# Moving a kernel's tokens and output rows by a table of row numbers: two batches and one output through GpSimd's indirect transfers, one batch at offsets in registers

## The reference, cut to what matters

```
x  = L0_attn_x
xn = layernorm(x)
x  = x + L0_attn(xn) + L0_ffn(xn)
#   L0_attn: 16 heads of 64, attention over channels: softmax(q k^T * 8) v, then w_out
#   L0_ffn:  64 experts of inner width 88, 8 chosen per token, and a shared expert: silu(x Wg) * (x Wu), then Wd
xn = layernorm(x)
x  = x + L1_attn(xn) + L1_ffn(xn)
#   L1_attn: for each of 8 heads the 32 nearest of the last 64 positions, weighted by exp(-distance)
#   L1_ffn:  relu(x W1 + low rank)^2, then W2, with ternary weights
return x
```

## Time and profile before

| | before |
|---|---|
| median time of 2 runs | 679.18 us (678.78 to 679.58) |
| span of the profiled execution | 676.3 us |
| instructions in it | 14256 |
| moved by transfers | 15.81 MB, nearly all in the first 45 us |

### The profile page before, as it was taken

One profiled execution on the slowest core, in us unless ns is written; L12 is line 12 of the kernel. 1 busy time (PEld: TensorE's weight loads), 2 busy tenths in 40 slices (PEclk: granted clock), 3 DMA queues, 4 the chain that ended last, 5 costly groups with the idle time before them and its releaser, 6 DMA issues.

```text
span 676.3 us, 14256 instructions
## 1 busy us (share of the span) xinstructions
PE 638.7 (94%) x4792; PEld 430.7 (64%) x4792; DVE 545.1 (81%) x2461; ACT 444.6 (66%) x802; POOL 365.4 (54%) x448
## 2 busy tenths in 40 slices
PE   4887999999999999999999999999999999998886
PEld 3544766667656666767567567666567776675675
DVE  5987778645975999997976899965485999967997
ACT  3674454646787957448587786455888956467953
POOL 2278366566462787665452886653763576621220
PEclk9999999999999999999999999999999999999999
DMA  8940000000000000000000000000000000000000
GB/s 297 392 131 1 0 1 0 1 0 1 0 1 1 2 2 1 1 1 1 2 0 2 2 1 2 1 1 1 1 1 1 2 1 1 1 1 17 18 18 17
DMA packets 12968, 15.81 MB, mean 23 GB/s; under 512 B 1728, under 2 KB 10832, under 8 KB 12384
## 3 DMA queue, kind: packets, MB, share of 16 engines
q1 hardware_dynamic: 12896, 14.91, 6.3%
HBM read 13.85 MB, written 1.05 MB: 22 GB/s over the span
## 4 chain that ended last, share of the span: by engine, by line
PE 61%; DVE 24%; ACT 7%; POOL 4%; issue 3%; DMA 0%; DVEq 0%; POOLq 0%; ACTq 0%
PE bank_A L522 17%; PE bank_U L522 14%; PE bank_G L522 14%; PE bank_X L522 14%; DVE Wk L1278 6%; DVE m L1275 5%; DVE S L859 4%; DVE GWk L859 2%; POOL PR L1654 2%; ACT L1350 1%; PE bank_X L531 1%; ACT Ed L1345 1%; PE bank_X L825 1%; ACT PR L1345 1%; ACT L1345 1%
## 5 line engine op out<-in xcount | busy, mean ns | idle before, releaser
L1654 POOL TENSOR_TENSOR Wlo<-Wgu,Whi 128x256 fp32r<-128x256 f32 x184 | 134.9, 743 | 119.5 <-ACT Whi L1345 116.5
L522 PE MATMUL bank_A<-S,WdT 128*128 128x512 f32 x346 | 172.2, 599 | 0.2 <-POOL S L1654 0.2
L1654 POOL TENSOR_TENSOR S<-S,Rb 128x512 f32<-128x512 f32 x84 | 108.6, 1294 | 72.0 <-DVE S L859 71.4
L859 DVE TENSOR_TENSOR S<-S,bank_U 128x512 f32<-128x512 f32 x173 | 116.6, 684 | 37.5 <-PE bank_U L522 23.3
L1345 ACT ACTIVATE Whi<-Wgu 128x256 fp32r<-128x256 f32 x184 | 73.0, 413 | 53.0 <-PE bank_U L522 48.5
L522 PE MATMUL bank_G<-xH,Whi 128*128 128x512 f32 x184 | 94.7, 515 | 8.0 <-POOL Wlo L1654 3.8
L522 PE MATMUL bank_U<-xH,Whi 128*128 128x512 f32 x184 | 93.4, 508 | 1.6 <-DVE wT L859 1.1
L522 PEld LDWEIGHTS bank_A<-S,WdT 128*128 128x128 f32 x346 | 61.7, 189 | 34.6 <-issue 21.4
L1278 DVE MATCH_REPLACE8 Wk<-m,Wk 128x79 f32<-128x79 f32 x384 | 82.2, 226 | 0.0
L1345 ACT ACTIVATE bank_G<-bank_G 128x512 f32<-128x512 f32 x83 | 48.4, 583 | 42.9 <-PE bank_G L522 42.6
L1345 ACT ACTIVATE S<-bank_G 128x512 f32<-128x512 f32 x90 | 53.7, 596 | 34.3 <-PE bank_G L522 27.5
(11 more groups left out here) (294 smaller groups left out, 1176.0 us busy)
## 6 DMA issues: line engine op xcount, KB each, us to landing
Wgu<-in_Wgu SPq DMA_DIRECT2D x2, 2048.0 KB, 14.4
xs<-in_x SPq DMA_DIRECT2D x4, 256.0 KB, 6.0
wqk<-in_w_qkv SPq DMA_DIRECT2D x1, 1024.0 KB, 6.9
Wgu<-in_Wgu SPq DMA_DIRECT2D x1, 1024.0 KB, 9.5
out<-xs SPq DMA_DIRECT2D x3, 256.0 KB, 2.3
Wgu<-in_Wgu SPq DMA_DIRECT2D x1, 512.0 KB, 4.7
wout<-in_w_out SPq DMA_DIRECT2D x1, 512.0 KB, 8.1
wvT<-in_wvT SPq DMA_DIRECT2D x1, 512.0 KB, 9.2
```

Of the source, the lines that this page charges most:

```text
L522: return engine.matmul(dst, lhsT, rhs, start=start, stop=stop)
L859: return engine.tensor_tensor(dst, a, b, op)
L1654: return engine.tensor_tensor(dst, a, b, op)
```

## The change

A table `rows` of shape (128, 16), the numbers 0 to 2047 in uint32, comes in as an input and is loaded into the tile `rowno`: column c holds the numbers of the 128 rows of tile c.

- Batch 1: SyncE reads the first row number of each of the four tiles from `rowno` into a register and issues one transfer of 64 KB at that offset; VectorE waits for 64 on `ld_x1`.
- Batch 2: GpSimd issues four indirect transfers, each of 128 rows named by a column of `rowno`.
- Batch 3: GpSimd zeroes batch 3's part of `xs` (ident minus ident), and later issues four indirect transfers that add the rows to it.
- Batch 0's output: four indirect transfers of GpSimd write the rows; SyncE stores batches 1 to 3 as before.
- SyncE no longer loads batches 2 and 3 and no longer stores batch 0.

```diff
@@ ORDER["pool"]: x and o are new letters (fetch three times, rows_out once)
-        "llylllllalmmlllmaaaclacalamlllmalmllmllmyylmlllmllmllmllmlymlllmmllmlllmlllmllmllmllmlylylmlllmllmll"
+        "llylllllalmmlllmaaaclacalamlllmalmllmllmyylmlllmllmllmllmlymxlllmmlxlmlllmxlllmllmllmllmlylylmlllmll"
...
+        rowno = sb("rowno", [128, B * NT], mybir.dt.uint32)
...
             load("ld_c", cst[:, :], d["consts"])
+            load("ld_r", rowno[:, :], d["rows"])
...
             load_w(2)
-            load_x(1)
+            sp.wait_ge("ld_r", 16)
+            for i in range(NT):
+                at = engine.value_load(rowno[0:1, NT + i:NT + i + 1], min_val=0, max_val=B * T - 128)
+                load("ld_x1", xs[:, NT + i, :], d["x"].rearrange("b t c -> (b t) c")[bass.ds(at, 128), :])
             load_w(3)
             load_w(4)
-            load_x(2)
-            load_x(3)
...
             def store(b, i, n):
                 j = i + n - 1
+                if b == 0:
+                    return
...
-            sp.wait_ge("st_out", 16 * (B - 1 + NT))
+            sp.wait_ge("st_out", 16 * (B - 2 + NT))
+            sp.wait_ge("st_rows", 16 * NT)
...
-                dve.wait_ge(f"ld_x{b}", 16)
+                dve.wait_ge(f"ld_x{b}", 16 * NT if b > 0 else 16)
...
+            def rows_of(b, i):
+                return bass.IndirectOffsetOnAxis(ap=rowno[:, NT * b + i:NT * b + i + 1], axis=0)
+
+            def fetch():
+                x = d["x"].rearrange("b t c -> (b t) c")
+                for b in (2, 3):
+                    if b == 3:
+                        yield
+                        po.wait_ge("ld_c", 16)
+                        one = K("ident").unsqueeze(1).to_broadcast([128, NT, 128])
+                        tt(xb(b), one, one, ALU.subtract).then_inc(sems("x_zero"), 1)
+                    yield
+                    po.wait_ge("ld_r", 16)
+                    if b == 3:
+                        po.wait_ge("x_zero", 1)
+                    for i in range(NT):
+                        engine.indirect_dma_start(
+                            out=xs[:, NT * b + i, :], out_offset=None, in_=x[:, :], in_offset=rows_of(b, i),
+                            **({"compute_op": ALU.add} if b == 3 else {})).then_inc(sems(f"ld_x{b}"), 16)
+
+            def rows_out():
+                o = out.rearrange("b t c -> (b t) c")
+                yield
+                po.wait_ge(empty(bank("dec", 0, NT - 1)), nth("dec", 0, NT - 1) + 1)
+                po.wait_ge(empty(bank("ff2", 0)), nth("ff2", 0) + 1)
+                for i in range(NT):
+                    engine.indirect_dma_start(
+                        out=o[:, :], out_offset=rows_of(0, i), in_=xs[:, i, :], in_offset=None).then_inc(sems("st_rows"), 16)
```

More of the change, by code:

```diff
@@ L71 @@
     "pool":
-        "llylllllalmmlllmaaaclacalamlllmalmllmllmyylmlllmllmllmllmlymlllmmllmlllmlllmllmllmllmlylylmlllmllmll"
-        "mhllmlymhlllmllmlmllmlaqllmqallaamqllamplalamlqllmlmlmqlplalmllqmlqlmllmlpmllqllmllmylylplmlhllmlmly"
-        "mhllllmmllllaqllaammlaqmlmlalaqlalmlapmllqmlqlmllmllqmplllmlqmllmlmllqllpmlllmlamplhlaaamallaalmlmha"
-        "lllmlmllmllqmlllqlmlqmllmlplmqlllmqmlllpmllqmllmqmlllpmmqphhhqqqqqqqq",
+        "llylllllalmmlllmaaaclacalamlllmalmllmllmyylmlllmllmllmllmlymxlllmmlxlmlllmxlllmllmllmllmlylylmlllmll"
+        "mllmhllmlymhlllmllmlmllmlaqllmqallaamqllamplalamlqllmlmlmqlplalmllqmlqlmllmlpmllqllmllmylylplmlhllml"
+        "mlymhllllmmllllaqllaammlaqmlmlalaqlalmlapmllqmlqlmllmllqmplllmlqmllmlmllqllpmlllmlamplhlaaamallaalml"
+        "mhalllmlmllmllqmlllqlmlqmllmlplmqlllmqmlllpmllqmllmqmlllpmmqphhohqqqqqqqq",
 }
@@ L1779, in every @@
                     yield from part(b)
-            weave("pool", c=zeros(), l=splits(), m=tiles(), y=every(route), a=every(attend), h=every(head), q=every(weights), p=adds())
+            weave("pool", c=zeros(), x=fetch(), o=rows_out(), l=splits(), m=tiles(), y=every(route), a=every(attend), h=every(head), q=every(weights), p=adds())
         block = ctx.enter_context(nc.Block())
@@ L1827 @@
         "x": i["L0_attn_x"],
+        "rows": np.arange(B * T, dtype=np.uint32).reshape(B * NT, 128).T,
         "consts": constants(),
```

## The result

| | before | changed |
|---|---|---|
| median time of 2 runs | 679.18 us | 698.16 us (696.70 to 699.63) |
| ratio | | 1.028, 95% interval 1.022 to 1.033 |
| span of the profiled execution | 676.3 us | 698.1 us |
| TensorE's hole ahead of chunk 32 / of chunk 40, as the ledger below counts it | none | 5.2 / 6.4 us |

The changed kernel is 19.0 us slower, 2.8%. Forecast were 10.8 us; the time lies inside the range, near its top. Run once more beside other runs of the kernel before it took 698.00 us, ratio 1.027 (1.025 to 1.030).

The account below looks back on a forecast made before the run. TensorE was taken as the bound from 100 to 610 us, so holes add to the time. First place 5.0, second 4.1 and clock 1.7 sum to 10.8 us on 679.2: 690.0 us, range 682.5 to 701.

Parts of the forecast that it names:

- D: Time for which one indirect transfer holds GpSimd; taken as 1.29 us, between ends of 0.44 and 2.35.
- First place: Batch 2's four transfers between product S3 and the Wlo of chunk 32; TensorE loses 5.0 us.
- (a): At chunk 32, GpSimd's hold makes Wlo late, so TensorE is late by 4D - 0.20, 4.96 us.
- (b): At route(2), VectorE's bn_stats wait for all four batch 2 transfers to land, making TensorE late by 4.76 us.
- cheap rival: GpSimd's transfers: issuing is nearly free (D = 0.44), about 2.3 us in all, 681.5 us; chance 0.20.
- Second place: Batch 3's four adding transfers after product S1, before the Wlo of chunk 40; 4D - 1.10, +4.1 us.
- Clock: TensorE's granted clock falls behind the holes; one drop counted, +1.7 us, none and two kept for the range.
- Zeroing: GpSimd's pass over batch 3's tile, 1.29 us, hidden in 2.58 us of idle time before a Wlo; cost 0.
- Output rows: Batch 0's four stores on GpSimd between hg and hq, with room for 3.25 us; cost 0 up to D = 1.65.
- SyncE's queue: Early table load and batch 1's register reads and four issues on SyncE, hidden; cost 0.
- Rival 1: GpSimd holds each transfer much longer (D = 2.35, or adding ones dearer), with two clock drops: 702.9 us; chance 0.30.
- Rivals 2, 3 and 4: 2: issuing nearly free, 681.5 us, chance 0.20; 3: slow SyncE register reads, 696.8, 0.03; 4: faster, 665.6, 0.01.

Follow-up runs that it names:

- e11: Kernel before with only batch 2's tokens by GpSimd's four indirect transfers, 64 rows each, SyncE loading the other halves; 686.99 us, ratio 1.0111.
- e2: Kernel before with only batch 3's part of the change: the zeroing and four adding transfers, placed as in the changed kernel; 689.01 us, ratio 1.0141.
- e12: Kernel before with only batch 3's zeroing and four adding transfers, one ahead of each of four Wlo; 683.51 us, ratio 1.0050.
- e14: All of the change, with the table loaded later and GpSimd's zeroing and batch 2 and 3 transfers moved to later waits than in an earlier idle-places version; 678.90 us, ratio 0.9997.
- e3: Kernel before with only batch 0's output rows stored by GpSimd's four indirect transfers; 679.25 us, ratio 0.9999.
- e5: Kernel before with only batch 3's tokens by GpSimd at the changed kernel's place, copying instead of adding, without zeroing; 683.07 us, ratio 1.0073.
- e13: Kernel before with only two tiles of batch 2 by GpSimd's indirect transfers, SyncE loading the other two; 682.94 us, ratio 1.0061.

## Why the prediction was right, and where it was off

The time lies in the range, but on its upper side: slower by more than 2% had a chance of 0.33, within 2% of 0.66. The range reached that far through its edge (D = 2.2 and two drops), so part of its being right is luck; two terms were mis-sized and two were put at nothing.

**First place.** Forecast 4D - 0.20 with D = 1.29, so +5.0; measured 5.17, 5.14, 5.08 and 5.10 in four profiles, D = 1.285. The slack of 0.20 was hardly there: 0.14 us lie between the end of Wlo and the matmul in the changed kernel too (122.88, 123.02). That the nearest row, GpSimd's pass over 128x512, gave D to a hundredth is luck: e11 shows that it isn't a cost per element or row. The choice of (a) over (b) was right, with the landing 1.5 us behind the last issue (122.12 to 123.60) for the 1.6 assumed. The Trainium skill's rule (DMA: Bandwidth & Descriptors, Anatomy of one DMA — SWDGE (gpsimd) path) of a small time for descriptors would have made this place nearly free; the trace disagrees for GpSimd's own time, and the prediction's cheap rival falls with it.

**Second place.** Forecast 4D - 1.10 = +4.1 "if adding costs GpSimd no more than copying". It does: 0.59 a transfer, so 6.4. With copying the step holds (4.20). This is the first mis-sized term, 2.3 us.

**Clock.** "I count one drop, +1.7 us", with two for the range. There were two, of 2.4 and 1.9: 4.3, so 2.6 us more than forecast, mostly for the second drop. The size came from a hole of 2.07 us ahead of other work; behind the holes of 4.9 to 6.6 us a drop cost 1.3 to 2.6, over eight holes in six profiles. The step also read from one profile that the hole of 2.61 us at 57.28 keeps the fast level; in nine of fourteen profiles the same hole lost it, and the hole of 2.07 us itself lost it in only five of the eleven profiles that have it.

**Zeroing.** Forecast 0, as hidden in GpSimd's idle time. GpSimd's time was hidden; what was overlooked is VectorE, which it blocked for 0.8 us ahead of a chunk whose Wlo had nothing to spare: 0.6.

**Output rows, SyncE's queue.** Forecast 0 and 0; measured alone 0.2 and 0.4 us with intervals that hold zero. Right, but for the open 2.3 us near the end, which come up only in the changed kernel. In its profile SyncE's later long issue is 6.57 us for the 9.79 of before, so the delay did come out of that standing.

**Sum.** 5.2 + 6.4 + 4.3 + 0.6 = 16.5, and with the open 2.3 it is 18.8, against 19.0 and 18.7 measured. That it comes so near is no proof of the 2.3: the parts measured alone give 18.6 without it, because their medians hold variation (e2's is 9.9 where its profile has 8.5). The forecast's 10.8 lacked 2.3 for adding, 2.6 for the clock, 0.6 for the zeroing and the 2.3 of the end. Rival 1 (a longer hold, 702.9) has half the truth: "the adding ones dearer" and "two drops" are in it, D = 2.35 isn't. Rivals 2, 3 and 4 fall by D = 1.285, by a read of about 0.8 us, and by the result.

## What to carry to other kernels

A transfer that GpSimd issues costs GpSimd its own time, about 1.3 us for each instruction here, with 64 rows as with 128, and 0.6 more if it adds; look for what GpSimd owes other engines in that time. Put such steps where the trace shows the engine idle and the next product early: the same change cost 18.7 us with two blocks of transfers ahead of late products, and nothing that could be told at idle places. Where TensorE is the bound, each hole of 4.9 us or more here cost 1.3 to 2.6 us again by the clock. Four transfers spread over four chunks (e12) lost 2.4 us where one block lost 7.9, hole and clock together; most of that is slack that each chunk has of its own. And a pass in an engine's idle time can still block another engine, as the zeroing did VectorE.

## What the runs showed of the hardware that I had not expected

- An indirect transfer takes GpSimd 0.95 us plus 0.30 between two, for 128 rows of 512 bytes as for 64 (0.90); the first of a block takes 1.17. Adding: 1.54 to 1.75 in the record, of which the last 0.55 overlaps and slows the next operation (three Wlo 2.68 instead of 2.11). Single ones can take longer: an adding one 2.09 in e14, a store 1.75 in e3.
- By idle time of TensorE, five holes of 4.4 to 4.6 us and three of 5.8 to 6.0 all brought the granted clock to 0.50, and one of 3.6 (e5) left it at 1.00. Short holes go either way in the same work: the one of 2.6 us at 57 to 59 us brought it down in nine of fourteen profiles, where it cost 0.3 to 0.4 us, once 1.3; the one of 2.07 near the end did so in five of eleven; one of 2.05 (e13) didn't.
- The clock can also stand at 0.50 for 3.4 us with no hole near it, as from 241.5 us on in the changed kernel, behind 16 matmuls of one column; it is in some executions of a kernel and not in others, and costs 1.1 us.
- A small VectorE operation waits out a whole pass of GpSimd: 128x8 elements took 0.97 us instead of 0.17 beside a pass of 1.04 us.
